# Expert slots of a mixture-of-experts layer, handed out in three phases instead of one

## What is computed

```python
x = x + conv_attention(ln_c(x))            # (8, 64, 16, 16)
t = to_tokens(x)                           # 2048 tokens x 64
u = ln_t(t).reshape(-1, C)
logits = u @ router_w.T                    # 8 experts
topk_probs, topk_idx = top_k(softmax(logits), 2)
topk_probs = topk_probs / (topk_probs.sum(-1, keepdims=True) + 1e-9)
h = silu(einsum('nc,ehc->neh', u, w1)) * einsum('nc,ehc->neh', u, w3)    # H = 682
y = einsum('neh,ech->nec', h, w2)
out = einsum('ne,nec->nc', gates, y)       # gates: the two probabilities, else 0
t = t + out
```

## Time and profile before

| what | value |
|---|---|
| median of 3 runs | 228.65 us (226.25 to 230.2) |
| the profiled execution | 226.59 us |
| its span, first to last instruction | 224.9 us |
| TensorE busy | 154.0 us (69%) |
| VectorE busy | 112.0 us (50%), 398 instructions |
| GpSimd busy | 85.5 us (38%) |
| mean granted clock of TensorE | 0.79 of full speed |
| moved by DMA | 33.47 MB, mean 149 GB/s |

### The profile page before, as it was taken

The page is one execution under the profiler, slowest core; times in us unless marked ns, Lnnn a source line. Parts: engine busy times, 40 slices in busy tenths (PEclk is TensorE's granted clock), DMA queues, the critical chain, the costliest instruction groups (busy, mean ns, idle before and its releaser), DMA issues.

```text
span 224.9 us, 4952 instructions
## 1 busy us (share of the span) xinstructions
PE 154.0 (69%) x1714; PEld 134.1 (60%) x1714; DVE 112.0 (50%) x398; ACT 72.3 (32%) x154; POOL 85.5 (38%) x109
## 2 busy tenths in 40 slices
PE   2647698795835000009999999999999999974040
PEld 2436598694734000007888888888888888862020
DVE  2696687679458640003544555454554545440050
ACT  2226544433001000005444445355444445530010
POOL 6142520204787777710003344333333444352300
PEclk9999755569555555555999999999999999997555
DMA  4999800000000000011067887887878887000153
GB/s 130 431 388 421 342 0 3 0 0 0 26 26 28 30 24 25 29 39 34 3 224 227 265 286 250 292 282 245 270 241 253 265 262 266 24 15 12 38 170 89
DMA packets 16315, 33.47 MB, mean 149 GB/s; under 512 B 7827, under 2 KB 9011, under 8 KB 15779
## 3 DMA queue, kind: packets, MB, share of 16 engines
q1 hardware_dynamic: 14018, 30.80, 40.6%
q0 software_dynamic: 2272, 2.36, 3.2%
HBM read 25.94 MB, written 7.21 MB: 147 GB/s over the span
## 4 chain that ended last, share of the span: by engine, by line
issue 40%; POOL 31%; DVE 11%; PE 9%; DMA 4%; ACT 3%; POOLq 1%; ACTq 0%; SPq 0%
POOL ys L335 16%; POOL xs L294 13%; PE bank L804 2%; DVE xn L478 2%; DMA y_in<-ys 2%; DVE kq_right L510 1%; DVE neg_max L515 1%; PE bank L754 1%; PE bank L770 1%; POOL rstd L278 1%; DMA x_sb<-x_tok 1%; ACT kq_right L355 1%; DMA ys<-y_out,y_row 1%; PE bank L792 1%; DVE t_sb L535 1%
## 5 line engine op out<-in xcount | busy, mean ns | idle before, releaser
L335 POOL DMA_INDIRECT ys<-y_out,y_row x39 | 37.5, 962 | 76.2 <-DVE y_out L722 70.2
L918 PE MATMUL bank<-x_cols,weights 64*128 64x128 f32 x468 | 64.5, 286 | 0.5 <-issue 0.5
L920 PE MATMUL bank<-x_cols,weights 64*128 64x128 f32 x468 | 64.5, 286 | 0.0
L714 DVE TENSOR_TENSOR hid<-bank,act_sb 128x512 f32<-128x512 f32 (+1 forms) x60 | 40.7, 678 | 45.8 <-ACT act_sb L429 36.9
L918 PEld LDWEIGHTS bank<-x_cols,weights 64*128 64x128 f32 x468 | 56.9, 193 | 7.4 <-issue 7.0
L920 PEld LDWEIGHTS bank<-x_cols,weights 64*128 64x128 f32 x468 | 56.9, 193 | 0.0
L429 ACT ACTIVATE act_sb<-bank 128x512 f32<-128x512 f32 (+1 forms) x60 | 35.3, 589 | 43.1 <-PE bank L918 42.3
L294 POOL DMA_INDIRECT xs<-rows,pos x32 | 31.2, 975 | 9.7 <-issue 9.7
L936 PE MATMUL bank<-hid,weights 128*64 128x128 f32 x468 | 30.8, 277 | 3.5 <-ACT y_cols L437 3.5
L936 PEld LDWEIGHTS bank<-hid,weights 128*64 128x64 f32 x468 | 25.8, 137 | 6.1 <-issue 3.8
L898 PE MATMUL bank<-ident,x_pairs 128*128 128x128 f32 x39 | 9.2, 317 | 26.7 <-issue 26.7
(11 more groups left out here) (123 smaller groups left out, 192.5 us busy)
## 6 DMA issues: line engine op xcount, KB each, us to landing
weights<-experts SPq DMA_DIRECT2D x39, 576.0 KB
xs<-zeros SPq DMA_DIRECT2D x4, 1056.0 KB, 8.8
x_in<-xs SPq DMA_DIRECT2D x39, 33.0 KB, 1.7
y_in<-ys SPq DMA_DIRECT2D x4, 256.0 KB, 4.0
ys<-y_out,y_row POOLq DMA_INDIRECT x39
xs<-rows,pos POOLq DMA_INDIRECT x32
out<-result SPq DMA_DIRECT2D x8, 64.0 KB, 2.1
x_sb<-x_tok SPq DMA_DIRECT2D x1, 384.0 KB, 3.6
```

The lines of the kernel that those rows point to most:

```text
L335: nc.gpsimd.indirect_dma_start(ys, bass.IndirectOffsetOnAxis(ap=y_row[:, HALVES * i + h:HALVES * i + h + 1], axis=0), y_out[:, i % RING, h ...
L714: nc.vector.tensor_tensor(live(i, hid[:, g % HRING, :]), live(i, H3_BANK[g % 3][:]), live(i, act_sb[:, g % 3, :]), ALU.mult).then_inc(hid_ ...
L918: first_ = nc.tensor.matmul(H1_BANK[g % 2][:, dst], weights[0:C, slot, at:at + P], x_cols[0:C, i % 2, src], start=True, stop=True)
L920: second_ = nc.tensor.matmul(H3_BANK[g % 3][:, dst], weights[C:P, slot, at:at + P], x_cols[C:P, i % 2, src], start=True, stop=True)
```

## The change

The slots are handed out in three phases. Phase 0 has slots 0 to 7, phase 1 slots 8 to 15, phase 2 slots 16 to 38. Phase 0 is worked out when two blocks (half of the tokens) are counted, phase 1 at three blocks, phase 2 at all four. In phases 0 and 1 only full subtiles are given out: 2048 rows over 8 experts make at least 9 full ones, 3072 rows at least 17. `full` is, per expert, the full subtiles so far less those already given (`used`); in phase 2 a last part-filled one counts too. The number of slots stays 39.

The fixed slots 0 to 7 are gone, so the first eight weight loads, too, come from `table`. They stand behind the wait for the first table. `dispatched` becomes three semaphores: phase 0's rows wait for the 16 scatters of blocks 0 and 1, phase 1's for the 8 of block 2, phase 2's for the 8 of block 3.

The first table (12 instructions and one for the count) stands on VectorE between `positions(2)` and `choose(3)`. The second and third (47 instructions with their bookkeeping) are spread over the first six pairs of the expert loop. TensorE's `rank` has one small matmul more at blocks 2 and 3, ScalarE loads the table for silu ahead of the loop. The diff, cut to its core:

```diff
+KNOWN = (2, 3, NBLK)
+PHASES = len(KNOWN)
+OPENED = (0, 8, 16, NS)
...
-            for e in range(E):
-                sp.dma_start(weights[:, e, :], experts[e]).then_inc(w_loaded[e], 16)
-
-            sp.wait_ge(dispatched, 16 * TILES * K_TOP)
-            for j in range(E):
-                sp.dma_start(x_in[:, j // HALVES, j % HALVES, :], xs[CAP * j:CAP * j + SUB, :]
-                             ).then_inc(x_in_loaded[j // HALVES], 16)
-            sp.wait_ge(table_ready, 1)
-            for i in range(E // HALVES, NT):
...
+            def load_weights(i, owners):
+                if i >= WSLOTS // HALVES:
+                    sp.wait_ge(hid_used, STEPS * (i - WSLOTS // HALVES + 1))
                 for h in halves(i):
                     s = (HALVES * i + h) % WSLOTS
                     sp.dma_start(weights[:, s, :], experts[bass.ds(owners[h], 1)].rearrange("o p c -> p (o c)")
                                  ).then_inc(w_loaded[s], 16)
+
+            for p in range(PHASES):
+                blocks = KNOWN[p] - (KNOWN[p - 1] if p else 0)
+                sp.wait_ge(table_ready, p + 1)
+                for i in pairs_of(p):
+                    owners = [sp.value_load(table[0:1, 0, HALVES * i + h:HALVES * i + h + 1],
+                                            min_val=0, max_val=E - 1) for h in halves(i)]
+                    at = [sp.value_load(table[0:1, 1, HALVES * i + h:HALVES * i + h + 1],
+                                        min_val=0, max_val=E * CAP - SUB) for h in halves(i)]
+                    if p == 0:
+                        load_weights(i, owners)
+                    if i == pairs_of(p)[0]:
+                        sp.wait_ge(dispatched[p], 16 * TPB * K_TOP * blocks)
+                    if i >= XRING:
+                        sp.wait_ge(gated, i - XRING + 1)
+                    for h in halves(i):
+                        sp.dma_start(x_in[:, i % XRING, h, :], xs[bass.ds(at[h], SUB), :]).then_inc(x_in_loaded[i % XRING], 16)
+                    if p > 0:
+                        load_weights(i, owners)
...
-                            rows[:, TPB * k + t, c, :], None).then_inc(dispatched, 16)
+                            rows[:, TPB * k + t, c, :], None).then_inc(dispatched[phase_of(k)], 16)
...
+            nc.scalar.preload_act_table(ACT.Silu)
...
+            def subtiles_of_experts(p):
+                dve.wait_ge(counts_ready, p + 1)
+                last = p == PHASES - 1
+                dims = [P, E, MOST]
+                chain(nc.vector.scalar_tensor_tensor(out=over[:], in0=taken_by[:, p, :].unsqueeze(2).to_broadcast(dims),
+                                                     scalar=float(SUB - 1) if last else 0.0,
+                                                     in1=steps_sub[:].unsqueeze(1).to_broadcast(dims),
+                                                     op0=ALU.add, op1=ALU.is_ge))
+                chain(nc.vector.tensor_reduce(full[:], over[:], AX.X, ALU.add))
+                if p > 0:
+                    chain(nc.vector.tensor_tensor(full[:], full[:], used[:, p - 1, :], ALU.subtract))
+                chain(nc.vector.tensor_tensor(upto_full[:], upto[:], full[:].unsqueeze(1).to_broadcast([P, E, E]),
+                                              ALU.mult))
+                chain(nc.vector.tensor_reduce(ends[:], upto_full[:], AX.X, ALU.add))
+
+            def owners_of_slots(p):
+                own = slice(OPENED[p], OPENED[p + 1])
+                n = OPENED[p + 1] - OPENED[p]
+                chain(nc.vector.tensor_scalar(given[:], ends[:], float(SUB), None, ALU.mult))
...
+                chain(nc.vector.tensor_reduce(owner[:, own], passed[:, own, :], AX.X, ALU.add))
+                nc.vector.tensor_copy(table[:, 0, own], owner[:, own]).then_inc(dve_step, 1)
+                steps[0] += 1
+                chain(nc.vector.tensor_tensor(starts[:, own, :], passed[:, own, :], end, ALU.mult))
+                chain(nc.vector.tensor_reduce(first[:, own], starts[:, own, :], AX.X, ALU.max))
+                chain(nc.vector.tensor_tensor(row_at[:, own], slot_at[:, own], first[:, own], ALU.subtract))
...
             positions(NBLK - 2)
+            subtiles_of_experts(0)
+            owners_of_slots(0)
+            rows_of_slots(0)
             choose(NBLK - 1)
             weigh(NBLK - 1)
             positions(NBLK - 1)
-            tile_table()
+            dve.wait_ge(counted, 1)
+            count(PHASES - 1, U_BANK[:, 0:E])
...
+            def tables_between(i, s):
+                if (i, s) == (0, 0):
+                    used_up(0)
+                    subtiles_of_experts(1)
+                elif (i, s) == (0, 1):
+                    owners_of_slots(1)
+                elif (i, s) == (1, 0):
+                    rows_of_slots(1)
+                elif (i, s) == (1, 2):
+                    used_up(1)
+                elif (i, s) == (2, 1):
+                    subtiles_of_experts(2)
+                elif (i, s) == (3, 0):
+                    owners_of_slots(2)
+                elif (i, s) == (4, 0):
+                    rows_of_slots(2)
+                elif (i, s) == (5, 0):
+                    occupancy(2)
...
                     multiply(STEPS * i + s)
                     if s == 0 and i + 2 < NT:
                         pair_up(i + 2)
+                    tables_between(i, s)
```

More of the change, by code:

```diff
@@ L30 @@
 CAP = B * N
-NX = (K_TOP * CAP - 1) // SUB
-NS = E + NX
+NS = E + (K_TOP * CAP - 1) // SUB
 NT = -(-NS // HALVES)
-MORE = CAP // SUB - 1
+MOST = CAP // SUB
+KNOWN = (2, 3, NBLK)
+PHASES = len(KNOWN)
+OPENED = (0, 8, 16, NS)
+assert all(OPENED[p + 1] <= -(-(K_TOP * BLK * KNOWN[p] - E * (SUB - 1)) // SUB) for p in range(PHASES - 1))
 RW = C + 2
@@ L114, in metaformer @@
         share = sb("share", [P, TILES])
[L116 to L128 removed]
+        taken_by = sb("taken_by", [P, PHASES, E])
+        over = sb("over", [P, E, MOST])
+        full = sb("full", [P, E])
+        upto_full = sb("upto_full", [P, E, E])
+        ends = sb("ends", [P, E])
+        given = sb("given", [P, E])
+        used = sb("used", [P, PHASES, E])
+        begin = sb("begin", [P, E])
+        left = sb("left", [P, E])
+        passed = sb("passed", [P, NS, E - 1])
+        starts = sb("starts", [P, NS, E - 1])
+        owner = sb("owner", [P, NS])
+        first = sb("first", [P, NS])
+        of_owner = sb("of_owner", [P, NS, E])
+        starts_e = sb("starts_e", [P, NS, E])
+        owned = sb("owned", [P, NS])
+        row_at = sb("row_at", [P, NS])
+        limit = sb("limit", [P, NS])
+        table = sb("table", [P, 2, NS], I32)
         keep = sb("keep", [P, NS], I32)
@@ L180, in metaformer @@
         zeros_made, xs_cleared = sem("zeros_made"), sem("xs_cleared")
-        dispatched = sem("dispatched")
-        counted = sem("counted")
+        dispatched = [sem(f"dispatched{p}") for p in range(PHASES)]
+        counted, counts_ready = sem("counted"), sem("counts_ready")
         keep_ready, table_ready = sem("keep_ready"), sem("table_ready")
@@ L212, in tiles, with phase_of, pairs_of @@
             return slice(TPB * k, TPB * (k + 1))
+        def phase_of(k):
+            return next(p for p in range(PHASES) if k < KNOWN[p])
+        def pairs_of(p):
+            return range(-(-OPENED[p] // HALVES), -(-OPENED[p + 1] // HALVES))
         block = ctx.enter_context(nc.Block())
@@ L314, in _ @@
             count_up(base[:], [[CAP, E]], 0, 0)
[L315 to L317 removed]
+            count_up(steps_sub[:], [[SUB, MOST]], SUB, 0)
+            for p in range(PHASES):
+                count_up(slot_at[:, OPENED[p]:OPENED[p + 1]], [[SUB, OPENED[p + 1] - OPENED[p]]], 0, 0)
             count_up(slot_no[:], [[1, 1]], 0, 1)
@@ L584, in positions @@
                 rank = K_BANK[:, 0:TPB * E].rearrange("p (t e) -> p t e", e=E)
+                for p in range(PHASES - 1):
+                    if KNOWN[p] == k:
+                        count(p, K_BANK[:, TPB * E:(TPB + 1) * E])
                 nc.vector.tensor_tensor(place[:], chosen[:, tiles(k), :, :],
@@ new lines, in used_up @@
+            def used_up(p):
+                chain(nc.vector.tensor_scalar(given[:], ends[:], float(OPENED[p + 1] - OPENED[p]), None, ALU.min))
+                before_ = slice(0, E - 1)
+                if p == 0:
+                    chain(nc.vector.tensor_copy(used[:, p, :], given[:]))
+                else:
+                    chain(nc.vector.tensor_tensor(used[:, p, :], used[:, p - 1, :], given[:], ALU.add))
+                chain(nc.vector.tensor_tensor(used[:, p, 1:], used[:, p, 1:], given[:, before_], ALU.subtract))
@@ L841, in rank @@
                                      start=False, stop=False)
+                if k in KNOWN:
+                    nc.tensor.matmul(K_BANK[:, TPB * E:(TPB + 1) * E], ones[:], carry[:, k, :], start=False, stop=False)
                 nc.tensor.matmul(K_BANK[:, 0:TPB * E], ones[:], carry[:, k:k + 1, :].to_broadcast([P, TPB, E]),
```

118 lines of the change are left out of this document (47 added, 71 removed).

## The result

The changed kernel takes 237.41 us (median of 4 runs, 237.37 to 238.83) beside 228.56 us of the kernel before (4 runs, 226.25 to 230.2): ratio 1.043, 95% interval 1.035 to 1.051. It is slower, where 219.5 was predicted. Its profiled execution has a span of 237.1 us. The medians here are of all executions; the ratios and their intervals leave out, on both sides, those that lie over 1.5% above the fastest of their kernel. Each series of runs has its own runs of the kernel before, whose median lies between 223.5 and 228.6 us, so times of different series are to be compared by their ratios.

What follows compares the result with a forecast made beforehand. TensorE bounds the loop (5.02 us a pair); before it, first loads wait for all 32 scatters. Gain 16.0 - 6.4 - 2.1 = 7.5 us from 226.59 gives 219.1, plus 0.4: 219.5; own range 216 to 223, overall 213 to 226.

Steps and rivals of the forecast that it cites:

- (2): SyncE: 2.4 us of register loads per pair, pairs 4.3 us apart; weights of pair 0 at 78.6, rows at 84.2.
- rival D: Dense tables: 0.5 us for each of 47 table instructions, 1 to 2.5 us gained, 224 to 226; chance 0.14.
- (1): First table on VectorE: 12 dependent instructions at 0.36 us each, 4.4 us, ready at 75.8.
- (3): Start: rows at VectorE to first up product 1.55 us; up products start at 85.9, 16.0 us earlier.
- (4): Pairs 0 to 5: TensorE waits on VectorE's products among table instructions, 6.4 us lost; pair 2 at 102.7.
- (5): Second table opens x_in 4, rows at 107.1; TensorE waits until about 111.2, pair 4 starts at 113.6.
- (6): Third table, 23 slots: VectorE 5.5 us a pair, up 13 waits 1 us, up 16 0.7; pair 6 at 124.8.
- The tail: The work behind the expert loop, forecast to stay as it is.
- C: Slower clock: TensorE rests in pairs 0 to 5, low clock at 9.75 us a pair, 239; chance 0.07.
- E: First loads held in the queue behind the scatters GpSimd goes on issuing, arriving with the last; 228; chance 0.02.
- The early silu table: Further edit: loading the silu table earlier than beside the first products, counted as costing nothing.

Runs made afterwards that it cites:

- The early scatters: Kernel before, with eight more scatters (zeros to rows of ys overwritten later) on GpSimd at 27 to 37 us; 226.77 us, ratio 1.007.
- holding the scatters: Changed kernel, GpSimd issuing the scatters of blocks 2 and 3 only after pair 3's rows landed; 232.79 us, ratio 1.038.
- the scatters spaced by waits: Changed kernel, third block's scatters two by two as rows of pairs 0 to 3 land, fourth block's one per step 7 to 14; 214.63 us, ratio 0.962.

## Why the prediction was wrong

**The step that failed is (2), the price of SyncE's instructions.** I took 2.4 us of register loads for a pair and 4.3 us from pair to pair, from issues at 101.82 to 115.79, behind the last scatter. In the changed kernel they run beside the scatters, at 0.70 us an instruction or more: from the table at 75.7 to the weights of pair 1 at 103.20 it took 27.5 us, where 7.1 were counted. I named register loads that cost more as what would make it wrong, but gave no rival to it. The price was in the trace of before: the gaps in VectorE's table. I read them as the cost of small table instructions and carried them into steps 1 and 6 and into rival D. The early scatters showed the same table without them, and holding the scatters brought the four pairs back to within 0.5 us of the predicted issues.

**(1) The table** came at 75.7, 75.8 predicted, but by two errors that cancel: its 12 instructions took 2.8 us, not 4.4, and began 1.5 us later.

**(3)** From rows to first product it was 1.65 us in place of 1.55. The start was late only because of step 2.

**(4)** was right where it could be seen. In the changed kernel TensorE first waited for pair 1's rows and worked 5.0 us in all between 77.2 and 109.1; but from pair 2's rows to pair 2's up products it took 10.0 us, 9.8 predicted, and with the scatters held pair 2 started at 102.53, 102.7 predicted.

**(5) and (6)** had two terms too large. They put 2.1 us of stalls between pairs 2 and 6. In the changed kernel the third table is worked there, and pair 6 starts 20.07 us after pair 2, four times 5.02, with no stall. With the scatters spaced by waits the times are near (85.22, 85.9 predicted; pair 2 at 102.79, 102.7; pair 4 at 112.82, 113.6; pair 5 at 119.23, 119.3; pair 6 at 124.24, 124.8), and this is partly luck. There is no stall before pair 4, and the one of 1.4 us before pair 5 is not the table's: VectorE waits until 112.06 for pair 5's rows. So a gain up to pair 6 was there, 8.1 us where 7.5 was the sum, in that one execution.

**The tail** was called unchanged. Between the two profiled executions the span fell by 11.8 us, 3.7 more than at pair 6. But they are of different series, whose kernel before took 228.56 and 223.49 us; within the series the gain is 8.9. In the trace a part of the 3.7 lies at the end of the loop, where ScalarE waits for the down products of the last but one pair. In the kernel before they end at 200.98:

```profile
204.11 0.27 ACT L437 COPY y_cols<-bank 128x128 f32<-128x128 f32 x1 [4.12 <-remote]
```

This update comes 2.9 to 3.3 us late in ten of the fourteen traces. In all ten GpSimd sends four scatters to `ys` there, 1.3 to 1.4 us apart. In the other four there is a pause in them, and it is 0.8 us late in three and 0.05 us in the kernel spaced by waits.

**The rivals.** The time is near C's 239, the mechanism isn't C's: the clock was low (granted 0.50 from 77.2 to 98.9), but TensorE worked only 4.8 us of that time and then waited for rows. It was low again at 0.60 on average from 115.0 to 123.5, where TensorE was busy for 7.0 of 8.5 us, but that is the low start that step 4 had counted in. The repeated fall that the Trainium skill describes (TensorE: Matmul & The Clock Gate, section HAM oscillation), each burst between waits starting slow again, is in this trace. The granted clock is 1.00 from 98.9 to 102.3, 0.50 from there to 109.1, and after this rest the products ran at 0.42 us each, where they take 0.27 at the full clock; after the next rest, from 113.1 to 116.5, they are at 0.42 again. From pair 2 on it stayed at 1.00, so C's six low pairs didn't come. E named the right culprit, the scatters, for the wrong victim: the second row load is recorded as issued at 93.33 and VectorE has the rows at 93.63. What was held was the issuing, and the semaphores. The early silu table, which I had costed at nothing, did not set the stretch off.

**What stays open** is what holds the others up. No row shows a busy resource: the scatters keep their 1.26 us, and their packets take about 0.05 us in the mean, in the slow stretch (77 to 98) as ahead of it. It might be a path that the engines' reports share with GpSimd's writing of its DMAs. It might be the recording itself. The Trainium skill, NOTIFIC — the notification-queue block, section Overflow: three behaviours, one of which stalls the engine, says that this block holds its producers back when its own pipeline is full, rather than lose a record. Two things in the traces point this way without showing it: SyncE's recorded issues in the stretch can come after the packets that they start, some 2 us late, and the one trace with nearly all updates of the row scatters has no slow stretch. That the other traces lack such records doesn't fit the page's sentence, unless they are lost elsewhere. Every run here has a recorded span beside its time, so none can separate the two, and how long the changed kernel takes when nothing is recorded is not known. Recording alone is not enough: in the loop TensorE executes 15 products a microsecond and as many weight loads (900 of each from 125 to 185), and no stretch comes. Nor was it tried which spacing is best, or the changed kernel beside the last one.

## What to carry to other kernels

A price read where an engine is alone holds there only: if a step is moved beside other work, look in the trace for how the same kind of instruction fares beside that work, and ask of each gap between cheap dependent instructions what else was running. A long row of GpSimd's indirect DMAs can hold up the instructions and semaphores of all the others, without harm as long as these have nothing to do; work that is to overlap it may need the row broken up, two scatters and then a wait for something that comes anyway, not a fill on GpSimd, which holds VectorE. When a change fails at one step, take that step's obstacle away before giving the change up: with sixteen scatters spaced out, this change measured 3.8% faster than the kernel before. And run the unmended kernel beside the mended one: without that it isn't shown what the mending did.

## What the runs showed of the hardware

- Beside an unbroken row of scatters (1.26 us each) SyncE's instructions moved in steps of 0.70 us, a register move 0.70 in place of 0.03, and a semaphore update of TensorE was seen 16 us late. It began 11 to 21 us into the first row, in one pair of executions sooner with more instructions on SyncE (69 in place of 75), 4 to 6 us into a row that followed a pause beside busy engines, and ended 2 to 5 us after the last scatter's start. One execution of the fourteen is an exception: sixteen scatters up to 76.60 and fourteen in a row from 115.23 to 131.92 slowed nobody.
- In the stretch the recorded time of an issue can be later than its effect: packets from 89.34 on, the issue at 90.53; in the kernel before they follow it by 0.9 us (98.16, 99.10).
- A pause of 3.2 us in the row was enough for some five scatters at normal pace. Sixteen scatters one in 1.84 us brought no slow stretch; four more behind them, one in 1.26 us, did.
- A memset of 0.70 us on GpSimd stretched a 128x256 copy on VectorE beside it from 0.29 to 0.90 us, one of 1.32 us such a copy to 1.36 us.
